# Attention operand stacks: part copies in blocks of 16 adjacent partitions instead of every sixth partition

## What is computed

```
x = x + 0.5 * ffn(layernorm(x))            # 256 -> 704 -> 256, inputs and weights rounded to FP4
x = x + attn(layernorm(x), Wq, Wk, Wv, Wo) # 8 batches, 16 heads, DH = 16, T = 1024
x = x + 0.5 * ffn(layernorm(x))

# attn, per batch b and head h
logits = einsum('bhqd,bhkd->bhqk', q, k) * DH ** -0.5
logits = where(causal_mask, neg, logits)
out    = einsum('bhqk,bhkd->bhqd', softmax(logits), v)
```

## Time and profile before

| | us |
|---|---|
| median of 3 runs | 2149.91 (2149.32 to 2154.04) |
| the profiled execution | 2154.04 |
| its span, first to last instruction | 2152.3 |
| PE busy | 2026.7 (94%) |
| DVE busy | 1888.4 (88%) |
| ACT busy | 1284.7 (60%) |
| POOL busy | 1042.1 (48%) |

### The profile page before, as it was taken

The page is one execution under the profiler, slowest core; times in us unless marked ns, Lnnn a source line. Parts: engine busy times, 40 slices in busy tenths (PEclk is TensorE's granted clock), DMA queues, the critical chain, the costliest instruction groups (busy, mean ns, idle before and its releaser), DMA issues. The chain is left out here.

```text
span 2152.3 us, 43595 instructions
## 1 busy us (share of the span) xinstructions
PE 2026.7 (94%) x13410; PEld 1320.9 (61%) x13410; DVE 1888.4 (88%) x4301; ACT 1284.7 (60%) x2138; POOL 1042.1 (48%) x1651
## 2 busy tenths in 40 slices
PE   4899999998998999999999999999998799999998
PEld 3688888887884333333333333333336688888887
DVE  6799999997987889898989998999955799999996
ACT  4455555544763577777777777777784355555552
POOL 5788888884655011111111111111111588888884
PEclk8899999999997899999999999999999999999999
DMA  6000000001685445555544554555426000000000
GB/s 198 20 0 0 0 0 0 0 1 66 227 258 155 103 123 133 129 135 141 137 126 126 132 132 128 140 141 135 108 73 203 11 21 19 19 19 19 19 15 25
DMA packets 163507, 184.98 MB, mean 86 GB/s; under 512 B 57696, under 2 KB 109280, under 8 KB 163040
## 3 DMA queue, kind: packets, MB, share of 16 engines
q1 hardware_dynamic: 160672, 182.11, 30.3%
q10 hardware_dynamic: 2688, 1.05, 0.2%
HBM read 113.90 MB, written 85.98 MB: 93 GB/s over the span
## 5 line engine op out<-in xcount | busy, mean ns | idle before, releaser
L1598 POOL TENSOR_SCALAR_AFFINE_SELECT diag_scores<-diag_scores 128x256 f32<-128x256 f32 (+1 forms) x192 | 95.0, 495 | 597.1 <-ACT diag_scores L1561 593.2
L1634 DVE CUSTOM_DVE_ANT_0 gu_ps<-gu_ps,mask_qk 128x256 f32<-128x256 f32 x511 | 291.7, 597 | 70.2 <-PE gu_ps L1421 68.5
L1563 ACT ACTIVATE probs<-hT_ps 128x512 f32<-128x512 f32 (+3 forms) x320 | 273.8, 856 | 127.5 <-PE hT_ps L1443 75.0
L1421 PE MATMUL gu_ps<-k_stack,q_stack 96*128 96x512 bf16 (+3 forms) x994 | 317.7, 347 | 21.9 <-DVE part_max L1634 8.6
L772 PE MATMUL gu_ps<-wguT_hi,ffn_xT_hi 128*128 128x512 f32 (+1 forms) x768 | 312.1, 406 | 6.4 <-ACT ffn_silu L732 5.8
L1462 PE MATMUL gu_ps<-probs,v_group 128*17 128x512 f32 (+3 forms) x3072 | 310.0, 490 | 2.6 <-ACT probs L1568 1.3
L772 PE MATMUL gu_ps<-wguT_hi,ffn_xT_lo 128*128 128x512 f32 (+1 forms) x768 | 289.8, 377 | 0.0
L772 PE MATMUL gu_ps<-wguT_lo,ffn_xT_hi 128*128 128x512 f32 (+1 forms) x768 | 289.1, 376 | 0.0
L750 ACT ACTIVATE ffn_z<-xs,ffn_shift,ffn_rstd 128x256 f32 (+1 forms) x128 | 77.0, 602 | 348.3 <-POOL ffn_shift L701 348.3
L1563 ACT ACTIVATE probs<-av_ps 128x512 f32<-128x512 f32 (+3 forms) x320 | 274.9, 859 | 0.6 <-PE av_ps L1443 0.5
L1421 PEld LDWEIGHTS gu_ps<-k_stack,q_stack 96*128 96x128 bf16 x994 | 91.5, 98 | 290.7 <-DVE part_max L1634 157.3
(11 more groups left out here) (190 smaller groups left out, 4977.6 us busy)
## 6 DMA issues: line engine op xcount, KB each, us to landing
q_stack<-q_parts SPq DMA_DIRECT2D x192, 128.0 KB, 3.4
k_stack<-k_parts SPq DMA_DIRECT2D x192, 128.0 KB, 3.5
o_all<-o_sb SPq DMA_DIRECT2D x64, 256.0 KB
q_parts<-qkv_parts SPq DMA_DIRECT2D x32, 384.0 KB, 2.7
k_parts<-qkv_parts SPq DMA_DIRECT2D x32, 384.0 KB, 2.8
v_ones<-qkv_vst SPq DMA_DIRECT2D x16, 544.0 KB, 4.0
v_group<-v_ones SPq DMA_DIRECT2D x32, 272.0 KB, 5.1
xs<-in_L_attn_x SPq DMA_DIRECT2D x8, 1024.0 KB, 7.5
```

The costliest lines, as they stand in the source:

```text
L1421: mm = T.matmul(out[:, e, :], qs[0:STACK, h0 + e, t * P:(t + 1) * P], ks[0:STACK, h0 + e, c * CHUNK:c * CHUNK + w], start=True, stop=True)
L1563: S.activation(probs[:, pair, i % 2, :, first:w], scores[pair][:, :, first:w], ACT.Exp, scale=DH ** -0.5).then_inc(s[pr], 1)
L1598: G.affine_select(out=block_of, in_=block_of, compare_op=ALU.is_ge, fill=MASKED, base=0, pattern=[[0, 2], [0, count], [1, P]], channel_mul ...
L1634: last = V.tensor_tensor_reduce(out=ps[:, e * w:(e + 1) * w], in0=ps[:, e * w:(e + 1) * w], in1=mask_qk[:, CHUNK - w:CHUNK], scale=1.0, sc ...
```

## The change

The loop in `fill` that issues the 12 transfers is unchanged in number, order, size and source. Only the destination partitions change. Before, slot s took the partitions s, s + 6, s + 12, ... s + 90, so that channel d of slot s was on partition s + 6d. Now slot s takes the 16 adjacent partitions from 16s on, and channel d is on partition 16s + d. q and k change in the same way, so each matmul still pairs the same rows and adds the same 96 products, in another order. The instruction streams of all five engines have the same rows as before.

```diff
-            slot, slots = 0, STACK // DH
+            at = 0
 
             for part, times in ((0, 3), (1, 2), (2, 1)):
                 for n in range(times):
-                    sp.dma_start(qs[slot:STACK:slots, :, :], q[part]).then_inc(stack_loaded[r], 16)
-                    sp.dma_start(ks[slot:STACK:slots, :, :], k[n]).then_inc(stack_loaded[r], 16)
-                    slot += 1
+                    sp.dma_start(qs[at:at + DH, :, :], q[part]).then_inc(stack_loaded[r], 16)
+                    sp.dma_start(ks[at:at + DH, :, :], k[n]).then_inc(stack_loaded[r], 16)
+                    at += DH
```

## The result

The changed kernel takes 2163.49 us (median of 4 runs, 2162.49 to 2164.6) against 2150.39 us for the kernel before (4 runs): the ratio of the times is 1.0052, with a 95% interval of 1.0040 to 1.0064. It is slower, as forecast, but by 11 us (by the ratio) to 13 us (by the medians) and not by 37. The two profiled executions are 2154.04 and 2163.68 us, 9.6 us apart. Executions of one kernel differ by several us among themselves (the kernel before took 2145.6 to 2157.6 in the later series), so stages are compared within traces here, and kernels by ratios taken on the same chip.

The account below looks back on a forecast made before the run. PE, nearly full, and DVE, tied through three PSUM banks, were taken as the bound. Projection 6 us plus groups 31 us made 37 us, on the median 2149.9 us: 2187 us; whole range 2148 to 2218, the forecast's own 2165 to 2215.

Parts of the forecast that it names:

- the rate taken for a fill, 107 GB/s: Drain rate of a fill's twelve transfers to adjacent partitions, taken between 180 and 96 GB/s; 14.7 us a fill.
- the delay d: How much later a fill drains, and so `sums` is issued: 14.7 - 8.7 = 6.0 us; 7.7 at the far end.
- The second rival: Fill's rate falls but stays above 116 GB/s, within the slack; only the projection loses, 2150 to 2155 us; chance 0.12.
- Term 2: Attention groups 1 to 28: DVE waits 1.5 us for `sums`, 1.1 us reaches PE in each; 31 us in all.
- the formula d - 4.9: Loss per attention group: the fill's delay less 4.5 us slack before the reciprocal and 0.4 us absorbed; 1.1 us forecast.
- the loop does not slip: In attention SP waits 1.6 us for `o_sb` before the next fill, so nothing slips beyond DVE's wait.
- its length less 0.4 us: In the groups, DVE's wait for `sums` reaches PE less 0.4 us absorbed before bank `xd_ps`; 1.1 of 1.5 us.
- Term 1: Mid-projection: ACT's 6.4 us wait for the v store behind group 0's fill grows by the whole delay, +6.0 us.
- The granted clock, kept at 0 in the sum: Projection: PE idle about 10 us could lower the clock; costed at 0, up to 8 us kept in the range.
- third: Far end: fill drains at 96 GB/s, 7.7 us later, groups lose 78 us in all; 2240 us; chance 0.12.
- fourth rival: Adjacent partitions drain the fill at issue rate, 206 GB/s, gaining in the projection; 2149 us, 2145 at best; chance 0.04.
- That the rate does not change: First rival: engines, not the destination, set the fill's drain rate; 2150 us; chance 0.20.

Follow-up runs that it names:

- all_but_first: Kernel before with 16 adjacent partitions in groups 1 to 31, every sixth partition kept in group 0's fill; 2162.95 us, ratio 1.0053.
- late_recip: Changed kernel with DVE's reciprocal of the sums one step later in each group (step 8 instead of 7); 2162.2 us, ratio 1.0043.
- late_inv_behind: Changed kernel with the reciprocal one step later and SP's load of the inverse behind the next group's first store; 2156.49 us, ratio 1.0018.
- first_only: Kernel before with 16 adjacent partitions in group 0's fill alone, the one inside the projection; 2154.52 us, ratio 1.0011.
- spread_first: Kernel before with group 0's fill issued two transfers at a time behind the stores of chunks 8 to 14; 2148.49 us, ratio 0.9985.
- split_fill: Changed kernel with only the first six transfers of a fill at the old place, the rest and v behind line 1264; 2241.67 us, ratio 1.0424.
- every_second: Kernel before with each copy going to 16 partitions two apart instead of six; 2151.68 us, ratio 0.9997.
- adjacent_covered: Changed kernel with group 0's fill spread over chunks 8 to 14, the reciprocal one step later and the inverse's load later; 2149.4 us, ratio 0.9976.
- k_three_on: Changed kernel with the k transfers rotated, so k of slot s + 3 follows q of slot s; 2154.11 us, ratio 1.0007.
- split_sixth: Kernel before, every sixth partition, with the second half of every fill moved behind line 1264; 2152.76 us, ratio 0.9998.
- inv_behind: Changed kernel with SP's load of the inverse of the sums only after the next group's first store; 2168.68 us, ratio 1.0083.

## Why the prediction was right or wrong

The mechanism stood: the drain rate falls with adjacent partitions, both places of loss are the two that were named, ACT's wait in the projection and DVE's new wait for `sums`, and PE and the start of attention cost nothing more. The time, 2163.5, is in the range of 2148 to 2218, but the size, 37 us, was three times too large. Two steps failed: the rate taken for a fill, 107 GB/s, and with it the delay d; and the pricing of the groups, which set one mean delay against one mean slack, 28 times over.

The rate measured 117 to 119 GB/s. The second rival had said that above 116 the groups lose nothing. Its condition came true and its outcome did not: the groups lost 6.9 us in one trace and 11.2 in the other. I had put the rate between its ends by the likeness of a row of another kind, a store from 64 partitions. The 104 GB/s of the Trainium skill (SBUF — State Buffer, section "Door 1: The DMA port swizzle") lay lower still; the measurement decides. At 118 GB/s the twelve transfers take 13.3 us, so d would be 4.6 us; the delay of `sums` came to 4.2 us, not 6.0. I also took SP's issue of 0.64 us a transfer as fixed by count and size, but it is 0.47 us with adjacent partitions. That moved little: the output store behind the fill is queued 8.9 us after the first load instead of 9.9 (means of 28 groups).

Term 2 was 31 us and measured 6.9 us in the 27 groups, in `all_but_first` 11.2. With a mean delay of 4.2 us and a slack of 4.4 to 4.5 in the mean, the formula d - 4.9 would have given none. Two things make up the rest. The issue of `sums` scatters over some 2 us from group to group, in the kernel before already (13.5 to 15.9 us after the first load), so single groups cross the edge; a mean hides that. And SP's round of the group closes. I had written that the loop does not slip; `late_recip` and `late_inv_behind` together show that it does. In the changed kernel itself SP finds no spare time before the next fill in 8 of 30 groups. What one wait costs, its length less 0.4 us, was right within 2 us for the sum of a trace: 5.9 against 6.9 us, and 9.7 against 11.2 in `all_but_first`.

Term 1 was 6.0 us and measured 2.5 us in ACT's wait and 2.4 in `first_only`. The v store of chunk 8, behind the fill, is issued 2.8 us later (612.29 instead of 609.46). Why the delay is smaller here than the 4.2 us of the groups stays open; the fill's rate before, 165 GB/s from 598.3 to 606.3 us, is inside the 155 to 180 of three fills in attention and does not explain it. That a wait's growth passes through whole was right. What I worked out as the loss before the change was too large: I took 8.75 us a chunk from chunks behind the stall, which were catching up. The undisturbed pace is 9.30 us, and the stall had cost 3.4 us, not 6.1.

The granted clock, kept at 0 in the sum, did fall behind the longer wait, to 0.50 for 3.4 us, once PE had been idle for 3.8 us:

```profile
619.50:623.30 3.80, 0.06 (x1) 0.00 (x0) 2.75 (x8) 3.48 (x8) 1.59 (x3) 1.00 1.09 387
623.60:627.00 3.40, 3.40 (x9) 2.63 (x9) 3.40 (x5) 2.96 (x6) 3.40 (x4) 0.51 0.68 241
```

In the kernel before it stayed at 1.00 there. The fall comes in all seven runs whose first fill goes in one piece to adjacent partitions and in none of the other six. It cost nothing that the stretch shows: this grew by 2.6 us and ACT's wait by 2.5. Of the third and fourth rival nothing was seen. That the rate does not change, at 0.20, is ruled out.

## What to carry to other kernels

Partitions that are neighbours are a bad target for a DMA of 16 partitions: the same bytes cost about twice the engine time, and a step of two was enough to cure it here. (The factor is an estimate: SP's queue took 40.2% of the engines' span instead of 30.3%, some 6.8 us more for each of 32 fills, and a fill at 118 GB/s takes 13.3.) Whether that costs time is decided by what stands behind on the queue, and by slack per iteration, its smallest values and not its mean, and after that by whether the issuing queue's round still fits in the iteration. A large transfer that need not be in one piece can be laid in small pieces behind other work, as `spread_first` did for 3 us.

## What the runs showed of the hardware

- Sixteen adjacent partitions as target: 117 to 119 GB/s at full share of all DMA engines. The same copies two or six partitions apart: 180 to 185 GB/s, held back by the issue. Two such blocks in alternation: 138 GB/s.
- SP issued a transfer to adjacent partitions in 0.43 us and one to stepped partitions in 0.59 us, whether the step was 2 or 6. I had expected no difference.
- A slow fill on SP's queue lengthened the landing of a 16 KB store on ACT's queue from 2.3 to 6.1 us (`split_fill`); with a spread one in the same place it landed after 2.7 us, and ACT had 5.6 us of waits in place of 106.7.
- Single groups of 30.2 us among groups of 28.79 occur in some traces without any DMA wait beside them. In each of them the granted clock fell to 0.50 for 3.4 us, and 3.4 us at the lower level cost 1.4 us. In `every_second`, the fall, the stretch before it and the same stretch one group earlier, where the clock stayed at 1.00:

```profile
962.00:965.00 3.00, 3.00 (x12) 0.58 (x5) 1.25 (x4) 1.79 (x4) 0.75 (x2) 0.50 0.35 96
957.00:961.00 4.00, 3.14 (x21) 1.02 (x20) 3.91 (x14) 2.08 (x4) 0.00 (x0) 1.00 0.91 214
928.00:932.00 4.00, 3.14 (x21) 0.96 (x19) 3.88 (x14) 2.08 (x4) 0.00 (x0) 1.00 0.72 219
```

  PE was busy 3.14 of 4 us both times, so why the clock fell in one group and not in the other stays open. Within the 27 groups there are three falls in `late_recip` and `adjacent_covered`, two in `k_three_on`, one in `first_only`, `every_second`, `split_sixth` and `late_inv_behind`, and none in the kernel before, the changed one, `all_but_first`, `inv_behind` and `spread_first`. These 1.4 us for each are to be taken off before sums over 27 groups are compared: `late_inv_behind` then stands at 777.9 us, `late_recip` at 782.2.
